# A second stage in a new order: PSUM banks reassigned, key norms on array quadrants, two modifiers in one product

## What is computed

```python
# token part, for each patch n
q, k, v = flat @ Wq[n] + bq[n], flat @ Wk[n] + bk[n], flat @ Wv[n] + bv[n]
attn = softmax(q k^T / sqrt(192)) v                # over the 64 images
att = layernorm(attn) * g + b + flat @ p1_w + p1_b
h = softmax(chain_of_five_layers(att) + att @ p2_w + p2_b)
# attention part: a recurrence over the 64 tokens of an image, 12 heads of 64
xn = layernorm(h)
k, v, q = [xn @ W.T + 0.1 * (gelu(xn @ w1.T + b1) @ w2.T + b2) for each of k, v, q]
k, v, q = layernorm of each, by head
for each token t:
    out_t = M q_t;  kn = k_t / (norm(k_t) + 1e-6);  pred = M kn
    M = M - (pred + lr * (pred - v_t)) kn^T
out = sigmoid(h @ Wg.T + bg) * (out @ Wo.T)
# feed-forward part
h2 = h + out; y2 = layernorm(h2)
result = h2 + layernorm(relu(y2 @ W1.T + b1) @ W2.T + b2 @ Wo + bo) * gamma + beta
```

## Time and profile before

| | us |
|---|---|
| median of 3 runs | 1339.08 (1338.1 to 1340.39) |
| the profiled execution, whole | 1343.92 |
| its span | 1342.0 |
| TensorE busy: products, weight loads | 1232.0 (92%), 986.8 (74%) |
| VectorE, ScalarE, GpSimd busy | 815.9 (61%), 726.8 (54%), 518.8 (39%) |

### The profile page before, as it was taken

How to read it: one execution, slowest core, us unless ns; L and a number is a source line. 1 busy time by engine, 2 the same in 40 slices (tenths; PEclk the granted TensorE clock), 3 DMA queues, 4 the chain that set the end, 5 groups by cost and what they waited for, 6 DMA issues and landing times.

```text
span 1342.0 us, 45313 instructions
## 1 busy us (share of the span) xinstructions
PE 1232.0 (92%) x17572; PEld 986.8 (74%) x17572; DVE 815.9 (61%) x2120; ACT 726.8 (54%) x1955; POOL 518.8 (39%) x689
## 2 busy tenths in 40 slices
PE   5898999999998588999999999999999999999975
PEld 5765666666665377888888888888888888888864
DVE  0136433333333266887877778787777878777752
ACT  0012222222222367777777777777777777777742
POOL 0000000000000355656565565556556555655521
PEclk8998999999998589999999999999999999999986
DMA  9888999999992012212221221122122112212210
GB/s 324 304 319 295 370 381 372 375 374 373 374 375 95 15 20 39 47 32 40 48 38 35 40 50 33 37 51 38 36 41 49 32 38 50 38 35 40 42 33 15
DMA packets 219995, 179.24 MB, mean 134 GB/s; under 512 B 164342, under 2 KB 189881, under 8 KB 219321
## 3 DMA queue, kind: packets, MB, share of 16 engines
q1 hardware_dynamic: 219818, 176.79, 41.3%
HBM read 154.72 MB, written 22.02 MB: 132 GB/s over the span
## 4 chain that ended last, share of the span: by engine, by line
PE 34%; POOL 31%; issue 25%; DVE 5%; SPq 2%; DMA 1%; ACT 1%; POOLq 0%; DVEq 0%; ACTq 0%
PE PS L438 29%; POOL region L1128 14%; POOL region L1111 5%; POOL region L1116 3%; POOL region L1122 1%; PE PS L514 1%; POOL region L1078 1%; POOL region L1094 1%; POOL region L1106 1%; SPq L308 1%; POOL region L1101 1%; PE PS L692 1%; PE PS L532 1%; PE PS L599 1%; POOL region L1091 1%
## 5 line engine op out<-in xcount | busy, mean ns | idle before, releaser
L438 PE MATMUL PS<-region 64*64 64x64 f32 (+6 forms) x5864 | 354.3, 287 | 20.7 <-DVE region L1176 13.6
L438 PEld LDWEIGHTS PS<-region 64*64 64x64 f32 (+3 forms) x5864 | 230.7, 139 | 119.6 <-issue 109.8
L1128 POOL TENSOR_TENSOR region<-region,powers 128x12 f32<-128x12 f32 x96 | 223.8, 2332 | 7.5
L1057 POOL TENSOR_TENSOR region<-region,powers 128x1 f32<-128x1 f32 x32 | 6.1, 192 | 408.5 <-DVE region L1236 408.5
L692 PEld LDWEIGHTS PS<-region 64*64 64x64 f32 x4608 | 145.1, 137 | 23.0 <-issue 18.9
L692 PE MATMUL PS<-region 64*64 64x64 f32 x4608 | 157.8, 223 | 1.4 <-ACT region L938 1.4
L438 PE MATMUL PS<-cw_hi,xr_hi 128*128 128x512 f32 (+3 forms) x384 | 149.3, 389 | 6.5 <-DVE region L1379 3.1
L905 ACT ACTIVATE region<-PS 128x512 f32<-128x512 f32 (+1 forms) x192 | 93.6, 488 | 84.3 <-PE PS L438 83.7
L438 PE MATMUL PS<-cw_lo,xr_hi 128*128 128x512 f32 (+3 forms) x384 | 130.8, 341 | 0.0
L438 PE MATMUL PS<-cw_hi,xr_lo 128*128 128x512 f32 (+3 forms) x384 | 130.5, 340 | 0.0
L832 ACT ACTIVATE region<-PS 128x384 f32<-128x384 f32 x32 | 15.7, 491 | 193.2 <-PE PS L438 193.2
(11 more groups left out here) (171 smaller groups left out, 2262.8 us busy)
## 6 DMA issues: line engine op xcount, KB each, us to landing
region<-in_Wq SPq DMA_DIRECT2D x32, 1152.0 KB, 5.8
region<-in_Wk SPq DMA_DIRECT2D x32, 1152.0 KB, 8.1
region<-in_Wv SPq DMA_DIRECT2D x32, 1152.0 KB, 7.7
region<-in_x SPq DMA_DIRECT2D x32, 384.0 KB, 6.7
n_scratch<-region SPq DMA_DIRECT2D x64, 192.0 KB, 3.4
region<-h_scratch SPq DMA_DIRECT2D x64, 96.0 KB, 2.0
region<-in_w SPq DMA_DIRECT2D x2, 2304.0 KB, 13.6
region<-i_scratch SPq DMA_DIRECT2D x256, 12.0 KB, 1.8
```

Source lines behind the costliest of these rows:

```text
L438: return nc.tensor.matmul(dst, lhsT, rhs, start=first, stop=last)
L1128: pool.tensor_tensor(rs[:, cols], rs_var[:, cols], root[:, cols], ALU.pow).then_inc(S["rs_ready"], 1)
```

## The change

All of it is in the second stage.

- **Order on TensorE.** Before, the projection pieces were spread over the step, between the products of tile k. Now pieces 1, 3, 0, 2, 4, 5 all stand in the first half, and `first_order`, `second_order` and half of `third_order` follow each other with nothing between. The other half of `third_order` opens the next step. `turn_kq` no longer stands right behind `ffn_first`; `ffn_first` and `ffn_second` moved ahead of `start_y`.
- **Banks.** `PIECE_BANK` goes from (0, 1, 0, 7, 7, 7) to (4, 7, 6, 0, 0, 1). `turn_x` writes bank 1 instead of 6, the modifiers bank 7 instead of 6, `turn_y2` and `ffn_first` bank 6 instead of 3, `ffn_second` bank 5 instead of 7. The protecting waits follow.
- **Key norms.** Six products of 128x128 weights with two columns become 24 of 64x64 weights with one column, on the four quarters, with a `settled` ahead and results in two banks. `take_norm` reads them in two copies.
- **Modifiers.** Three products of 48 columns for each half of the contraction become two, one of 112 columns (k and q side by side with a gap) and one of 48 (v): 4 products instead of 6.
- **ScalarE, VectorE, GpSimd, SyncE** get new orders. On VectorE `normalise` moves a step later, `gate_and_add` is split, `take_n` stands ahead of `take_a`. On GpSimd `key_lengths` is first and `input_rstds` near the end. On SyncE `gather_blocks` stands right behind `scatter_inverse`, and `store_result` comes a step later.

```diff
-PIECE_BANK = (0, 1, 0, 7, 7, 7)
+PIECE_BANK = (4, 7, 6, 0, 0, 1)
+PIECE_NTH = (3, 1, 4, 2, 5, 6)
...
             def modifier(x):
...
-                    for m in range(3):
-                        last = nc.tensor.matmul(PS[R2:R2 + MOD, 6, m * P:(m + 1) * P], w[:, m * MOD:(m + 1) * MOD],
+                    for i, (first, cols) in enumerate(((0, slice(0, MOD_PAIR)), (R2, slice(MOD_PAIR, MOD_PAIR + MOD)))):
+                        last = nc.tensor.matmul(PS[first:MOD_PAIR, 7, i * P:(i + 1) * P], w[:, cols],
...
             def key_norms(j):
...
-                    last = mm(PS[:, 6, 2 * i:2 * i + 2], ksq[:, i, :], head_ones)
+                    for e in range(2):
+                        tokens = slice(64 * e, 64 * e + 64)
+                        for odd, bank in enumerate((6, 3)):
+                            rows = slice(64 * odd, 64 * odd + 64)
+                            last = mm(PS[tokens, bank, NORM_AT + i:NORM_AT + i + 1], ksq[rows, i, tokens], head_ones[rows, odd:odd + 1])
...
             for s in range(-1, TILES + 5):
                 x, t, j, l, m = s, s - 1, s - 2, s - 4, s - 5
-                if live(x + 1):
-                    input_rstds(x + 1)
                 if live(j):
                     key_lengths(j)
+                if live(m):
+                    shifted_residual(m)
```

More of the change, by code:

```diff
@@ L415, in _ @@
             load_h(hp, "hp_in", 1)
-            for s in range(TILES + 5):
-                x, j, k, m = s, s - 2, s - 3, s - 5
+            for s in range(TILES + 6):
+                x, j, k, done = s, s - 2, s - 3, s - 6
                 if live(k):
                     scatter_inverse(k)
+                if live(j):
+                    gather_blocks(j)
+                if live(k):
                     need(sp, "h2_ready", k - 1)
@@ L426, in _ @@
                     load_h(hp, "hp_in", x + 2)
[L427 to L430, removed]
+                if live(done):
+                    store_result(done)
             sp.wait_ge(S["out0"], TILES // 2 * 16)
@@ L772, in _ @@
                 if live(j):
                     turn_kq(j)
+                if live(t):
+                    project(t, (1,))
+                if live(l):
+                    read_out(l)
+                if live(t):
+                    project(t, (3, 0))
+                if live(j):
+                    key_norms(j)
+                if live(l):
+                    weigh_out(l)
+                if live(t):
+                    project(t, (2,))
+                if live(x):
+                    turn_x(x)
@@ L774, in _ @@
+                if live(j):
+                    grams(j, 0)
+                    grams(j, 1)
+                if live(t):
+                    project(t, (4, 5))
+                if live(x):
+                    modifier(x)
+                if live(l):
+                    turn_y2(l)
+                if live(k):
+                    form_e(k)
                 if live(m):
@@ L776, in _ @@
                 if live(l):
-                    read_out(l)
-                if live(t):
-                    project(t, range(0, 1))
-                if live(j):
-                    key_norms(j)
-                    grams(j, 0)
-                    grams(j, 1)
-                if live(l):
-                    weigh_out(l)
-                if live(t):
-                    project(t, range(1, 3))
-                if live(x):
-                    turn_x(x, j)
-                if live(t):
-                    project(t, range(3, 4))
-                if live(k):
-                    form_e(k)
-                if live(x):
-                    modifier(x)
+                    ffn_first(l)
                 if live(k):
                     start_y(k)
-                if live(t):
-                    project(t, range(4, 5))
+                if live(x):
+                    gates(x)
                 if live(k):
@@ L1504, in _ @@
                     take_n(j, 1)
+                if live(l):
+                    norm_h2(l)
+                if live(j):
+                    take_a(j, 0)
+                    take_a(j, 1)
+                    right_side(j)
                 if live(k):
@@ L1508, in _ @@
                 if live(t):
[L1509 removed]
                     moments(t, 1)
[L1511 to L1512 removed]
+                if live(m):
+                    ffn_out(m)
+                if live(t):
+                    moments(t, 2)
+                if live(x + 1):
+                    moments_h(x + 1)
                 if live(x):
                     low_part(x)
[L1515 to L1520 removed]
                 if live(t):
@@ L1523, in _ @@
                     scale(t, 1)
-                    moments(t, 2)
                 if live(j):
```

215 lines of the change are left out of this document (111 added, 104 removed).

## The result

The changed kernel took 1290.43 us (median of 4 runs, 1286.69 to 1292.02) where the kernel before took 1339.74 in the same runs: a ratio of 0.9622 [0.9605, 0.9639], 49 us less. Measured again with the last experiments it took 1285.86. The profiled execution took 1291.68, its span 1289.7.

The account below looks back on a forecast made before the run. It took TensorE to bound the kernel; its terms summed to -2.01 us a step, taken as 1.95, times 28 steps 55 us, from 1343.9 to 1289, less 4.8 to 1284 us; range 1264 to 1314.

Parts of the forecast that it names:

- TensorE is therefore the bound: Second stage, kernel before: TensorE, 96% busy, sets the step, with 1.8 us of waits in 26.1.
- The waits and the uncovered copies: TensorE's waits ahead of `turn_kq`, piece 3 and key norms go (-0.82, -0.42, -0.18); uncovered copies cost +0.20 and +0.15.
- the 0.40 left in the sum: TensorE's wait ahead of `start_y` for `take_e`, kept at its old 0.40 us; ends 0 and 1.0.
- Key norms: On TensorE, 48 records in 0.79 us plus 0.10 for `settled` replace 1.43 us: 0.54 saved a step.
- Modifiers: On TensorE, eight records at 0.10 us plus 0.19 between halves replace 1.39 us: 0.40 saved a step.
- GpSimd is not late: `scale`, needed by `turn_kq`: GpSimd's second root is done about 3.6 us behind `take_e`, in time.
- hidden by 1.6: The blocks' way through DRAM takes 7.1 us; VectorE's inversion wants them 8.7 us behind `take_n`.
- The residual sum's lower end: VectorE's sum took 1.47 beside the mask; started first, it takes a quarter, and `start_y` waits 0.
- The slower rival: GpSimd's roots of 2.28 us block VectorE's `right_side` and `scale`s, costing 2.2 a step: 1345 us; chance 0.05.
- Another knot: Rival: banks or orders tie another knot, for instance a piece waiting for its bank; 1.0 of 1.95 lost, 1312; chance 0.09.
- 28 steps: 27 full steps plus ten partial ones counted as one, each saving 1.95 us: 55 us.
- From the profile to the median: The median of runs taken as 4.8 us below the profiled execution: 1289 becomes 1284.

Follow-up runs that it names:

- e4: The kernel before with the new small key norms alone: 1339.59 us, ratio 0.9999, step 26.14.
- e5: The kernel before with `ffn_first` between the halves of `third_order` and `relu` between ScalarE's two copies: 1340.87 us, ratio 0.9997, step 26.12.
- e9: The kernel before with `key_lengths` placed ahead of `input_rstds` on GpSimd, nothing else: 1320.96 us, ratio 0.9857, step 25.34.
- e1: The changed kernel with the old key norms (six products with two columns, no `settled` ahead): 1298.21 us, ratio 0.9688, step 24.56.
- e3: The changed kernel with both old key norms and old modifiers, leaving the new order and banks: 1304.65 us, ratio 0.9729, step 24.82.
- e7: The changed kernel with the value modifier's weights padded with zero columns from 48 to 112: 1280.25 us, ratio 0.9543, step 23.97.
- e8: The changed kernel with e7's padding, and the modifiers' second half padded with zero rows from 64 to 128: 1268.11 us, ratio 0.947, step 23.64.
- e2: The changed kernel with the old modifiers, three products of 48 columns for each half of the contraction: 1292.51 us, ratio 0.9644, step 24.47.
- e13: The changed kernel unedited, measured a second time: 1285.86 us, ratio 0.9597, step 24.22.
- e12: The changed kernel with e8's padding, and the second half of `ffn_first` padded from 64 to 128 rows: 1267.83 us, ratio 0.9466, step 23.63.

## Why the prediction was right, and where it was not

Predicted were 1284 us and a step of 24.2; measured 1290.43 (1285.86 in the second measurement) and 24.23. By its steps:

- *"TensorE is therefore the bound"*: wrong for the kernel before (e4, e5: shorter work of TensorE, no change; e9: a shorter chain off TensorE, -19 us), right for the changed one (e1 to e3 add up). I had set the chain of waits aside with "an engine at 60% that waits for others is no bound by itself". No engine was, but the two in turn were. The sum came out right since the change removes both limits: the input's roots leave the chain, `ffn_out` moves between the moments, the sum starts ahead of the mask; after that TensorE sets the step, and what I had counted on TensorE is what remains to be counted. That the change took the chain away too was luck as far as my working goes: it stands nowhere in the sum. (the earlier trace rows also has ScalarE at 76 and GpSimd at 59%, where I wrote 75 and 60.) For the edits of e4 and e5 the same working would have promised (0.54 + 0.82) x 28 = 38 us, and each shows none.
- *The waits and the uncovered copies*, -0.82 - 0.42 - 0.18 + 0.20 + 0.15 = -1.07: e3 measures -1.32. All three waits went. Of the difference 0.21 is `start_y`, which waits 0.19 and not the 0.40 left in the sum. The orders took 4.67, within the 4.6 to 5.0 said, but the +0.35 for uncovered copies did not come as I had it: the three took 1.49 + 1.48 + 1.48 = 4.45 before, so they grew by 0.22, while the idle time ahead of them fell from 0.36 + 0.20 to 0.23. Other changes of form moved as well (0.23 ahead of `read_out` is gone, 0.20 ahead of the grams is new); I had left them out of the sum, and no run parts them.
- *Key norms*, -0.54: -0.33. The 0.79 is exact; mis-sized is the `settled` ahead, 0.36 where I took 0.10. I had said that such gaps run up to 0.23, but the earlier trace rows has 0.36 ahead of `form_e` (821.53), and I had listed it myself. From the last load of a piece to `weigh_out` it is 1.35 (820.68 to 822.03) against 1.69 in e1 (796.16 to 797.85).
  The Trainium skill ("TensorEngine Tiling (Array Packing)", Instruction Overhead) gives each matmul about 60 cycles, an estimated 1.2 us for the 48 at 2.4 GHz. The row at 821.23 has 0.79 for them, so the estimate is too high where the four quarters take turns.
- *Modifiers*, -0.40: -0.24. Eight records take 1.15 and not 0.80, for in each half two loads of 112 columns are followed by two of 48, on average 0.147 a load; e7 and e8 take that away. With the 0.18 between the halves it is 1.33, against 1.39 for the twelve before: the records themselves save next to nothing. The gain lies ahead of them. A load of 112 columns follows the last one of a piece after 0.12 (828.87 to 828.99), one of 48 in e2 after 0.32 (801.88 to 802.20). From that last load to `turn_y2` it is 1.64 against 1.89.
- *"GpSimd is not late"*, *"hidden by 1.6"*: both held. `turn_kq` has no idle ahead of it, and the inversion starts right behind `scale` (837.75), 8.85 behind `take_n`, where I had 8.7 (the rounded terms as printed add to 8.5).
- *The residual sum's lower end* ("if VectorE starts first, it takes a quarter of that"): so it was, 0.36, and with it `start_y`'s wait fell.
- *The slower rival*, roots that block VectorE: no. `right_side` took 0.95 beside a root, as in the earlier trace rows. The opposite happens: beside the two `scale`s (835.99) GpSimd's L1142 takes 0.64 and L1148 2.86, where those beside no such operation take 0.21 and 2.28. It has the room. The Trainium skill ("SBUF — State Buffer", SBUF: two separate sides) gives the pair to whichever starts first, an operation of GpSimd or one of VectorE with two inputs in SBUF, for the whole instruction: mask and `scale` agree, the roots don't. *Another knot* didn't come either.
- *28 steps*: 53.5 us by the measured 1.91, and the spans differ by 52.3. The whole second stage kept to it but for its head: the second interval took 27.05 where 25.38 stood before, at a granted clock of 0.84 instead of 0.99 (500 to 525 us). In e1, e2, e5 that stretch shows 1.00, in e8 0.86, and the second interval of the same unedited kernel was 24.28 in e13. It varies from run to run; why stays open.
- *From the profile to the median*: I took 4.8 us off, as the profiled execution of before lay that much above its median. That of after lies 1.3 above it. This makes 3.6 of the 6.4 us missed; the rest is 52.2 us between the profiled executions (1343.92 - 1291.68) in place of 55.

## What to carry to other kernels

Before you add up the waits of the busiest engine, shorten its work by one edit: if the time stays, follow the idle times of two engines that wait for each other around one full period, and look for a link that needn't be in it. An edit that is worth nothing alone can be worth its full size once the other limit is gone, and the other way round. Where small products interrupt large ones, pad them with zeros to the form of their neighbours and time that too; once another engine sets that place, as in e12, it brings nothing more.

## What the hardware showed that I had not expected

- A product with fewer columns or rows can cost more. Two loads of 112 columns and two of 48 take 0.59 us, four of 112 take 0.51; going from 128 to 64 rows and back costs two gaps of 0.18. Padding saved 0.59 of a step (24.23 to 23.64).
- With four quarters in turn, a load record costs 0.0165 us on average (48 in 0.79) whether its product has one column or 64; a product has two such records.
- Operations of VectorE and GpSimd can hold each other: beside the mask of 768 a sum of 192 takes 1.47 and not 0.36; beside a `scale` of 768 GpSimd's sum of 12 takes 0.64 and not 0.21; a root of 12 holds nothing, though it runs 2.28. It isn't only operations with two tensor inputs that are held: in the changed kernel VectorE's first operation of the inverse norms (L1454, 12 columns, one tensor input, 824.86) takes 0.56 beside GpSimd's sum of 192 (L1126), where it took 0.17 before (818.78).
